# Attention products on quarter tiles, a new load order and new queue orders in an attention and expert block

## The reference

```python
qp = q @ Wq.T                                    # q: the first normalised x
k, v = jnp.split(latent_kv @ Wkv_expand.T, 2, axis=-1)
scores = jnp.einsum('bhqd,bhkd->bhqk', qh, kh) * inv_sqrt_d    # 512 x 64 for each head
attn = jax.nn.softmax(jnp.where(causal, scores, min), axis=-1)
out = jnp.einsum('bhqk,bhkd->bhqd', attn, vh) ... @ Wout.T
x = x + tanh(g_xattn) * out
x = x + tanh(g_ffn) * (two routed experts of normalised x + shared expert)
```

## Time and profile before

| what | value |
|---|---|
| median of the runs | 488.65 us |
| the profiled execution's own time | 488.76 us |
| its span in the profile | 487.0 us |
| PE, DVE, ACT, POOL busy | 88, 63, 51, 47% |
| granted PE clock, mean | 0.981 of full |

### The profile page before, as it was taken

How to read it: one execution, slowest core, us unless ns; L and a number is a source line. 1 busy time by engine, 2 the same in 40 slices (tenths; PEclk the granted TensorE clock), 3 DMA queues, 4 the chain that set the end, 5 groups by cost and what they waited for, 6 DMA issues and landing times.

```text
span 487.0 us, 7654 instructions
## 1 busy us (share of the span) xinstructions
PE 427.6 (88%) x2445; PEld 231.1 (47%) x2446; DVE 307.9 (63%) x659; ACT 249.9 (51%) x450; POOL 230.0 (47%) x205
## 2 busy tenths in 40 slices
PE   2599789998999989988897979889999999999981
PEld 1355435554555555554444435445455545544540
DVE  4788876888568885688767868963334334333330
ACT  3879565767537675376342526743343434343330
POOL 4007527541875417749152041855546455565422
PEclk9999989999999999999998899999999999999996
DMA  7920023241042253541642375866557656576453
GB/s 305 416 69 1 0 66 126 92 153 65 2 131 86 88 194 24 173 153 67 232 193 71 107 228 167 185 122 105 116 95 125 113 102 125 88 128 104 90 66 43
DMA packets 20478, 58.61 MB, mean 120 GB/s; under 512 B 3489, under 2 KB 3745, under 8 KB 19810
## 3 DMA queue, kind: packets, MB, share of 16 engines
q0 software_dynamic: 9504, 20.48, 23.7%
q1 hardware_dynamic: 10946, 37.77, 22.9%
HBM read 35.54 MB, written 22.70 MB: 120 GB/s over the span
## 4 chain that ended last, share of the span: by engine, by line
PE 66%; DVE 15%; ACT 6%; issue 5%; POOL 3%; DMA 3%; POOLq 0%; SPq 0%; DVEq 0%; ACTq 0%
PE bank L1554 56%; PE bank L1559 9%; ACT arena L656 4%; DVE arena L987 3%; DVE xn L1056 2%; POOL arena L555 2%; DVE x_sb L1034 1%; DMA xrows<-xn 1%; DVE mx L1094 1%; DMA rows<-xrows,entry 1%; DVE mv L1002 1%; DMA arena<-in_wkv 1%; POOL lists L533 1%; ACT arena L688 1%; DVE mx L1088 1%
## 5 line engine op out<-in xcount | busy, mean ns | idle before, releaser
L1554 PE MATMUL bank<-arena 128*128 128x512 f16 (+1 forms) x576 | 109.5, 347 | 3.4 <-DVE arena L987 1.6
L1554 PE MATMUL bank<-arena,GT 128*128 x468 | 107.4, 379 | 2.2 <-issue 2.0
L640 POOL DMA_INDIRECT out<-rows,entry x39 | 61.7, 1582 | 80.8 <-ACT rows L962 29.9
L1554 PE MATMUL bank<-arena,gT 128*128 (+1 forms) x330 | 80.2, 379 | 2.2 <-DVE gT L986 1.8
L1554 PEld LDWEIGHTS bank<-arena 128*128 128x128 f16 x576 | 55.9, 98 | 51.7 <-issue 3.9
L656 ACT ACTIVATE arena<-bank 128x512 f16<-128x512 f32 (+1 forms) x88 | 49.4, 586 | 47.8 <-PE bank L1554 29.1
L1554 PEld LDWEIGHTS bank<-arena,GT 128*128 128x128 f16 x468 | 45.8, 98 | 49.0 <-issue 2.9
L987 DVE SCALAR_TENSOR_TENSOR arena<-bank,arena 128x512 f16<-128x512 f32 (+1 forms) x72 | 45.8, 666 | 22.2 <-ACT arena L656 21.8
L616 POOL DMA_INDIRECT rows<-xrows,entry x39 | 39.3, 1008 | 37.0 <-DVE entry L1362 20.3
L986 DVE TENSOR_TENSOR GT<-bank,GT 128x512 f16<-128x512 f32 x39 | 26.9, 690 | 46.4 <-ACT GT L656 46.3
L1554 PE MATMUL bank<-arena,x2T 128*128 128x512 f16 x192 | 46.6, 395 | 4.1 <-DVE x2T L986 4.1
(11 more groups left out here) (169 smaller groups left out, 590.2 us busy)
## 6 DMA issues: line engine op xcount, KB each, us to landing
x_sb<-in_experts SPq DMA_DIRECT2D x9, 768.0 KB, 5.1
rows<-in_experts SPq DMA_DIRECT2D x6, 768.0 KB, 5.7
xrows<-xn SPq DMA_DIRECT2D x16, 256.0 KB, 2.4
out<-x_sb SPq DMA_DIRECT2D x16, 256.0 KB, 2.2
image<-GT SPq DMA_DIRECT2D x5, 768.0 KB, 4.1
arena<-image SPq DMA_DIRECT2D x10, 384.0 KB, 5.3
x_sb<-in_x SPq DMA_DIRECT2D x2, 1024.0 KB, 8.8
x_sb<-in_x SPq DMA_DIRECT2D x1, 2048.0 KB, 16.3
```

What stands on the lines that cost most here:

```text
L640: nc.gpsimd.indirect_dma_start(out=out, out_offset=bass.IndirectOffsetOnAxis(ap=entry[:, 1, j:j + 1], axis=0), in_=Y[:, j % RING, :], in_o ...
L1554: last = nc.tensor.matmul(dst, a, b, start=n == 0, stop=n == len(steps) - 1)
```

## The change

In words, by engine:

- SP: the rows of sample 0 are loaded first, in two halves, then `wq` in two halves, then context and key weights; the gates come after the rows of sample 1.
- Start: sample 0 is normalised by DVE (`first_norm`) and not by ACT; it is turned and half projected before the keys are made. `wq` is laid out by group and split in halves (`wq_low`, `wq_high`).
- Attention: `vbd`, `fill_v` and the memset of `vbd` go. `attend(b, g)` multiplies each head by itself, twelve matmuls a group: weights of 64 rows by 32 columns, 512 columns streamed; heads 0 and 2 of a group lie on partitions 0 to 63, heads 1 and 3 on 64 to 127, and head j writes partitions 32j to 32j+31 of the group's bank. Score products stay as they are.
- Sample 0: "p" turns come earlier in `MIX_FIRST`, the sums are pulled ahead, the split of the shared expert is behind or between.
- Second normalisation: the turn of `x2` tile 0 moves between `y` 2 and `y` 3 on PE; POOL waits for `xn2` before `softmax_sub` 1 and 2; `hidden(f, 0)` comes before `scores(c, 3)`.
- Samples 1 and 2: `router_place` and `head_sum` 2 come ahead of the mix, `image_rest` between `softmax_mul` 1 and 2.

The diff, cut to its core:

```diff
-        MIX_FIRST = (("q", 0), ("q", 1), ("v", 0), ("q", 2), ("v", 1), ("q", 3), ("p", 0), ("v", 2), ("p", 1),
-                     ("v", 3), ("p", 2), ("p", 3))
+        MIX_FIRST = (("q", 0), ("q", 1), ("v", 0), ("q", 2), ("p", 0), ("v", 1), ("q", 3), ("p", 1), ("v", 2),
+                     ("p", 2), ("v", 3), ("p", 3))
...
+            for n in range(2):
+                sp.dma_start(x_sb[:, 2 * n * D:2 * (n + 1) * D].rearrange("p (t d) -> p t d", t=2),
+                             x[:, 2 * n:2 * (n + 1), :]).then_inc(ld_x0[n], 16)
+            for n in range(2):
+                sp.dma_start(wq_raw[:, wq_half(n)], wq[:, wq_half(n)]).then_inc(ld_wq[n], 16)
             sp.dma_start(ctx_raw.rearrange("p (b e k) -> p b e k", b=B, e=2), ctx_rows).then_inc(ld_kv, 16)
             sp.dma_start(wkv_raw, wkv).then_inc(ld_kv, 16)
-            sp.dma_start(x_sb[:, 0:PER * D].rearrange("p (t d) -> p t d", t=PER), x[:, 0:PER, :]).then_inc(ld_x0, 16)
-            sp.dma_start(gl[:, 0:2], gates).then_inc(ld_gates, 16)
-            sp.dma_start(wq_raw, wq).then_inc(ld_wq, 16)
             sp.dma_start(x_sb[:, PER * D:2 * PER * D].rearrange("p (t d) -> p t d", t=PER),
                          x[:, PER:2 * PER, :]).then_inc(ld_x1, 16)
+            sp.dma_start(gl[:, 0:2], gates).then_inc(ld_gates, 16)
...
-            pool.memset(vbd[:, :].bitcast(F32), 0.0).then_inc(consts, 1)
...
-                elif prev is not None:
-                    image_rest(2 * b - 1)
                 for i in range(PER):
                     if not nxt and i == 3:
                         split_piece(1)
+                    if nxt and prev is not None and i == 2:
+                        image_rest(2 * b - 1)
                     softmax_mul(b, i)
...
                 if nxt:
                     softmax_mask(b + 1)
-                    image_rest(2 * b)
                     softmax_sub(b + 1, 0)
                 power2(b, 0)
                 if nxt:
+                    pool.wait_ge(xn2_ready, 4 * b + 2)
                     softmax_sub(b + 1, 1)
-                    softmax_sub(b + 1, 2)
+                    image_rest(2 * b)
                 else:
                     scatter_pairs(prev, (1,))
                 power2(b, 1)
+                if nxt:
+                    pool.wait_ge(xn2_ready, 4 * b + 4)
+                    softmax_sub(b + 1, 2)
...
-                turn_hi(c, "x2", 0)
+                turn_hi(c, "x2", 1)
+                tanh_h(f, 0)
                 scores_out(c, 3)
-                turn_hi(c, "x2", 1)
+                turn_hi(c, "x2", 2)
                 exps(c, 2)
...
                 if nxt:
                     image_high(2 * c - 1)
+                    exps(c, 3)
+                    norm1(f + 2, 0)
                 else:
...
-                if nxt:
-                    norm1(f + 2, 0)
-                    norm1(f + 2, 1)
-                fill_v(c, (0, 1))
                 tanh_h(f, 2)
-                fill_v(c, (2, 3))
...
+                    if nxt and i == 2:
+                        image_scale(2 * c - 1)
...
-                        if prev is not None and n == 1:
+                        if prev is not None and n == 2:
                             image_high(2 * b)
-                        if prev is not None and n == 2:
+                        if prev is not None and n == 3:
                             image_scale(2 * b)
+                    if prev is None and (kind, n) == ("v", 0):
+                        fill_k(1)
                 if prev is None:
-                    act.wait_ge(v_lo, B)
-                    fill_v(0, range(4))
-                    fill_k(1)
+                    shared_hi_half(0)
...
                     if prev is None:
+                        shared_hi_half(1)
+                    scores_out(b + 1, 1)
+                    if prev is None:
                         image_high(0)
-                        image_scale(0)
-                    scores_out(b + 1, 1)
                     exps(b + 1, 0)
                     scores_out(b + 1, 2)
+                    turn_hi(b + 1, "x2", 0)
+                    if prev is None:
+                        image_scale(0)
                     exps(b + 1, 1)
                 else:
                     copy_weights(prev)
                     for k in range(7, 10):
                         split_piece(k)
+                    turn_hi(b + 1, "x2", 0)
...
+                dve.wait_ge(ln1_power, 1)
+                for i in range(PER):
+                    V.tensor_scalar(xn1[:, i * D:(i + 1) * D], x_tile(i), ln1[:, i, 0:1], ln1[:, i, 2:3],
+                                    ALU.subtract, ALU.mult).then_inc(xn1_ready, 1)
...
+            dve.wait_ge(ld_x0[0], 16)
+            statistics1(range(2))
+            dve.wait_ge(ld_x0[1], 16)
+            statistics1(range(2, PER))
             aggregate1(0)
-            bias1(0)
-            dve.wait_ge(tanh_gates, 1)
-            V.tensor_scalar(gl[:, 0:1], gl[:, 2:3], 1.0 / (S_A * S_W), None, ALU.mult).then_inc(gates_ready, 1)
-            V.tensor_scalar(gl[:, 1:2], gl[:, 3:4], 1.0 / (S_G * S_W), None, ALU.mult).then_inc(gates_ready, 1)
-            dve.wait_ge(gates_ready, 2)
-            for g in range(NG):
-                dve.wait_ge(k_hi, g + 1)
-                lo(kc[:, 1, g].rearrange("p b k -> p (b k)"), mm_bank[g][:, 0:B * SK],
-                   kc[:, 0, g].rearrange("p b k -> p (b k)"), S_KV / (S_CTX * S_W)).then_inc(k_lo, 1)
-            dve.wait_ge(wq_hi, 1)
-            lo(wq_s[:, DC * D:2 * DC * D], wq_raw, wq_s[:, 0:DC * D], S_W).then_inc(wq_lo, 1)
+            own_block()
+            first_norm()
+            wq_low(0)
...
                 c = f + 1
-                if not isinstance(f, int) or f < B - 1:
-                    turn_lo(c, "x2", 0)
...
+                hidden(f, 0)
                 head_max(c, 3)
-                hidden(f, 0)
                 turn_lo(c, "x2", 2)
+                hidden(f, 1)
                 turn_lo(c, "x2", 3)
-                hidden(f, 1)
...
                     head_max(b, 3)
+                    aggregate1(2)
+                    head_sum(b, 0)
                 else:
                     feed_forward(prev, nxt)
+                    if nxt:
+                        router_place(prev)
+                        head_sum(b, 2)
                 for kind, n in mix(b):
                     if kind == "q":
                         project_lo(b + 1, n)
-                        if prev is None:
-                            head_sum(b, n)
+                        if prev is None and n < 2:
+                            head_sum(b, n + 1)
                     elif kind == "v":
                         values_lo(n)
+                        if n == 0:
+                            head_sum(b, 3)
                     else:
                         probabilities_lo(b, n)
                         if prev is not None and n == 0:
-                            head_sum(b, 2)
-                            router_place(prev)
-                        if prev is not None and n == 1:
                             head_sum(b, 3)
                 if prev is None:
-                    aggregate1(2)
                     shared_lo_half(0)
-                    shared_lo_half(1)
-                    dve.wait_ge(gate_hi, 1)
-                    lo(gate_s[:, 1].rearrange("p c e -> p (c e)"), gate_raw[:, :],
-                       gate_s[:, 0].rearrange("p c e -> p (c e)"), S_W).then_inc(gate_lo, 1)
-                    bias1(2)
...
-                x1_and_statistics(b, 0)
+                if prev is None:
+                    shared_lo_half(1)
+                    dve.wait_ge(gate_hi, 1)
+                    lo(gate_s[:, 1].rearrange("p c e -> p (c e)"), gate_raw[:, :],
+                       gate_s[:, 0].rearrange("p c e -> p (c e)"), S_W).then_inc(gate_lo, 1)
                 if nxt:
                     head_max(b + 1, 0)
+                x1_and_statistics(b, 0)
+                if prev is None:
+                    bias1(2)
+                if nxt:
                     head_max(b + 1, 1)
                 x1_and_statistics(b, 1)
                 aggregate2(b, 0)
                 norm2(b, 0)
+                x1_and_statistics(b, 2)
+                turn_lo(b + 1, "x2", 0)
                 if nxt:
                     head_max(b + 1, 2)
-                x1_and_statistics(b, 2)
-                if not nxt:
-                    turn_lo(b + 1, "x2", 0)
                 make_x1(b, 3)
...
+            wq_low(1)
             dve.wait_ge(ld_x1, 16)
-            statistics1(range(PER, 2 * PER))
+            statistics1(range(PER, PER + 2))
+            context_lo()
+            project_lo(0, 0)
+            statistics1(range(PER + 2, 2 * PER))
             aggregate1(1)
+            project_lo(0, 1)
             bias1(1)
-            project_lo(0, 0)
+            keys_lo()
             dve.wait_ge(wout_hi, 1)
             lo(wout_s[:, DC * D:2 * DC * D], wout_raw, wout_s[:, 0:DC * D], S_W).then_inc(wout_lo, 1)
```

(45 more changed lines are left out.)

164 lines of the change are left out of this document (88 added, 76 removed).

## The result

Four runs of the changed kernel gave 480.68 to 482.90 us, median 482.04; before, in the same comparison, median 488.2 (486.98 to 490.65). The ratio is 0.9865, 95% interval 0.9826 to 0.9903: 6.6 us faster by the ratio (6.2 by the medians), where 17.3 were forecast. The profiled execution took 482.76 us with 480.9 of span, against 488.8 and 487.0: 6.1 less of span.

What follows compares the result with a forecast made beforehand. It took PE's own work to set the pace in samples 1 and 2, with DVE next. Gains of 6.0 + 2 x (2.4 + 2.2) + (0.9 + 1.2) = 17.3 from 488.8 gave 471.5 us, range 464 to 483.

Steps and rivals of the forecast that it cites:

- start to products 0: From kernel start to sample 0's attention products: rows loaded first, probabilities turned earlier; 3.3 us gained.
- products 0 to `y` 0: Sample 0, attention products to output product: `y` at 66.8 where it was 72.8, 6.0 gained counted from the start.
- to products 1, to products 2: PE's gaps before the attention products of samples 1 and 2: 2.2 of 3.5 us a sample gained.
- products to `y`, samples 1, 2: Attention products to output product in samples 1 and 2: tiled products gain 2.4 us each.
- `y` 2 to products 3: Stretch before sample 3's attention products: the wait before `hidden` 0 goes, 1.2 of 5.3 us of gaps gained.
- products 3 to `y` 3: Sample 3, attention products to output product: only 0.9 us gained, since DVE is late next.
- The overlap: Attention products: four heads of a round run at once, 0.7 us a group, 2.8 a sample.
- no overlap: Rival: attention heads run one after another, 10.4 us a sample against 5.2; 500.4 us in all, chance 0.08.
- two at a time: Rival: attention products run in six rounds a group, 1.3 us as now; 479.6 us in all, chance 0.08.
- What follows them: Emptying of attention groups: DVE just keeps up, the next score products cover the last low half; samples 1, 2 gain 2.4 each.
- signs of being wrong: A group over 1.3 us, `y` 0 to `y` 1 over 59, or expert phase not moving by as much as sample 3's `y`.
- gaps stay: Rival: DVE or POOL stalls move without shrinking, only the attention products gain; 480.7 us in all, chance 0.16.

Runs made afterwards that it cites:

- control: The changed kernel with only GpSimd's tile number load asserted to lie in its bounds; 483.88 us, ratio to before 0.9893.
- short_stats: The changed kernel with the first normalisation's statistics of samples 2 and 3 reading 128 of 512 columns; 474.69 us, ratio to before 0.9734.
- muls_first: The changed kernel with GpSimd's four softmax multiplications ahead of both weight splits in the last sample; 481.41 us, ratio to before 0.9825.
- scatter_late: The changed kernel with GpSimd's eight list scatters of samples 1 and 2 moved behind `softmax_sub(b+1, 2)`; 495.23 us, ratio to before 1.0133.
- scatter_apart: The changed kernel with multiplications before splits, sample 3's statistics later, and the second four scatters moved one sample later; 483.74 us, ratio to before 0.9909.
- control_c: The same program as control, run again beside scatter_apart on one chip; 482.95 us, ratio to before 0.9897.
- whole_scatter_late: The changed kernel with 128x128 attention products over the filled `vbd` again and the scatters moved as in scatter_late; 504.08 us, ratio to before 1.0306.
- tiles_scatter_late: The kernel before with only tiled attention products and the scatters behind `power2(b, 1)`; 493.83 us, ratio to before 1.0110.
- whole_again: The changed kernel with 128x128 attention products over the filled `vbd`, its memset and `fill_v` put back; 484.72 us, ratio to before 0.9896.
- one_term: The changed kernel with attention products keeping the first of three terms, 16 matmuls in place of 48; 484.32 us, ratio to before 0.9940.
- drain_first: The changed kernel with PE waiting once for all four low halves of the next queries before attention in samples 1 and 2; 483.71 us, ratio 0.9884.
- short_stats_b: The same program as short_stats, run again on another chip; 479.19 us, ratio to before 0.9844.

## Why the forecast was half right

Each step against the profiled execution, in us of gain (a minus is a loss); the second column has the parts of the 17.3 with 6.0 cut at products 0 as the forecast has it (3.3 and 2.7):

| step | forecast | after | what the runs showed |
|---|---|---|---|
| start to products 0 | 3.3 | 1.7 | projection at 16.19 (16.5 forecast) |
| products 0 to `y` 0 | 2.7 | 2.6 | 3.5 where the clock held (control) |
| to products 1, to products 2 | 2.2, 2.2 | 0.3, 1.4 | 1.0, 2.0 in short_stats |
| products to `y`, samples 1, 2 | 2.4, 2.4 | -0.9, -1.3 | 2.6, 2.6 in short_stats |
| `y` 2 to products 3 | 1.2 | -1.4 | 0.7 in muls_first |
| products 3 to `y` 3 | 0.9 | 1.2 | |
| end | 0 | 2.5 | 0.8 in the control |
| sum | 17.3 | 6.1 | |

**The overlap was right.** Four heads run side by side: 0.69 a group where 0.7 was taken. The rivals "no overlap" and "two at a time" fall with sample 3. By the estimate from the Trainium skill, TensorE: Matmul & The Clock Gate, Part 3, it would have been 0.84 a group; the page's 3.07 times is measured for four row tiles, and is too little for these tiles of two row halves and four column strips: 10.4/2.77 is 3.75. Gotcha 1 of the Trainium skill's TensorEngine Tiling (Array Packing) does not hold for heads that share a bank and write different partitions.

**The step that failed is, under "What follows them", "So samples 1 and 2 gain 2.4 each"**: it took for granted that a product's signal arrives when the product is done. Beside GpSimd's scatters it did not, on four of the five chips of the experiments, and that made 7.0 of the 11.2 missed. Shown: the stand goes when the scatters go (scatter_late beside muls_first, scatter_apart beside control_c), moves with them to other products (scatter_late, whole_scatter_late, tiles_scatter_late), ends beside the attention products 1.4 to 1.6 us behind the last of eight, needs neither tiles nor density (whole_again, one_term) nor a full queue ahead (drain_first) nor a low clock (control), and is absent on one chip for the same program (short_stats and short_stats_b). Not shown: what is shared. The trace has no instruction fetch in the stand and DMA engines 1 to 3% busy in sample 1. Also open is why the kernel before, whose scatters ran from 123.74 to 133.81 beside whole products, has its signals in time in its one trace; its median, 487.7 to 489.2 on all chips, shows no sign of it, but a stand of 0.8 us a sample as in whole_again could hide there.

**The start: a term mis-sized.** The first three maxima end at 42.8, about as forecast (42.6). The list behind them misses one term (changed kernel, timelines of DVE and of POOL):

```profile
44.59 1.65 DVE L1052 TENSOR_SCALAR ln<-ln 128x8 f32<-128x8 f32 x1
```

```profile
40.59 7.48 POOL L562 TENSOR_TENSOR arena<-arena,mx 128x1024 f32<-128x1024 f32 x4 [3.16 <-DVE mx L1121]
```

The aggregate's last step, here on 8 columns, takes 0.17 us in the median of its line; here it lasts until the third of GpSimd's four subtractions is done (46.2): 1.5 of the 1.6 missed. I had used this very effect for the gap of `norm2`, which did go (1.00 a pair at 79.60 and 87.32), but had not looked for the places where the new order makes it.

**The gaps** of samples 1 and 2 shrank by 1.0 and 2.0 where no stand and no low clock lay ahead, so 2.2 each was somewhat too much; in the profiled run PE also waited 1.1 us for `xn` behind `y` 0; so do the other kernels whose products 0 take 4.46 us, and those with 2.77 wait 0.4. **Sample 3's** 1.2 turned into a loss by a reorder that I put at nothing: `direct_scale(0)` moved down ScalarE's list, GpSimd's split waits for it, and the first multiplication queues behind the split (the 1.97 above), on POOL in the changed kernel:

```profile
218.03 3.54 POOL L578 TENSOR_TENSOR arena<-x_sb,arena 128x384 f16<-128x384 f32 x4 [4.06 <-ACT x_sb L673]
221.52 5.63 POOL L569 TENSOR_TENSOR arena<-arena,rd 128x1024 f32<-128x1024 f32 x3
```

muls_first shows it.

**The end** gained 2.5 where nothing was forecast. In its first 54.8 us the granted clock was 0.97, where it was 0.94 in the kernel before and in the control; why it differs there is open. So 2.5 of the 6.1 is luck as far as the forecast goes.

**The signs.** Two of the forecast's own signs of being wrong came: from `y` of sample 0 to `y` of sample 1 it takes 61.7 us (over 59), and the end moved by 6.1 where `y` 3 moved by 3.6. The rival "gaps stay" came near the time (480.7 for 482.0) by luck: the gaps did shrink, and the products of samples 1 and 2 gained nothing.

## What to carry to other kernels

- Before you count on a faster stretch of TensorE, look at what GpSimd sends out beside it. Here scatters held back its signals, and in most traces its matmuls too; read it in the engine that waits, and measure on more than one chip, each time with a control on the same chip: one program differed by 4.5 us.
- A reorder that separates a VectorE operation from a GpSimd one at one place joins them at another. List the small operations of VectorE too against GpSimd's new timetable: 0.17 became 1.65, and 0.19 became 6.43.
- A split or a scaling moved down one engine's list delays whatever queues behind its consumer on the next one; follow the move across two queues.

## What the hardware did that I had not expected

On four of five chips signals of TensorE reached ScalarE up to 5.2 us late beside indirect DMAs of GpSimd, at the worst with matmul records that look done; the last held back was seen 1.39 to 1.62 us behind the last of eight. 48 tiled matmuls of 512 columns take 2.77 us; at 0.216 each one after the other they would take 3.75 times as long. A VectorE operation of 32 columns lasted 6.43 us beside GpSimd's eight subtractions. After 4.4 us without products TensorE's next stretch had a granted clock of 0.95 and took 57.35 us for 54.4.
